# GpSimd's high and low split in two column halves, in an attention and MLP kernel

## The reference

```python
x1 = layernorm(x)                        # 16 x 512 x 128
xn = layernorm(x1) * ln_g + ln_b
q, k, v = xn @ Wq + bq, xn @ Wk + bk, xn @ Wv + bv
content = einsum("bihd,bjhd->bhij", q + u_bias, k)
pos = relative_shift(einsum("bihd,jhd->bhij", q + v_bias, pe @ Wp))
attn = softmax((content + pos) * dh ** -0.5)
head = einsum("bhij,bjhd->bihd", attn, v)
h = relu(s0 * concat([x1, -x1]) @ sign(k0)) * 2
h = relu(s1 * h @ sign(k1)) * 2
out = x + head @ Wo + bo + s2 * h @ sign(k2)
```

## Time and profile before

| what | value |
|---|---|
| time, three runs | 1454.56, 1454.69, 1456.49 us (median 1454.69) |
| the profiled execution | 1453.06 us |
| its span, first to last instruction | 1451.2 us |
| granted TensorE clock, mean | 0.998 |
| busy: PE, DVE, ACT, POOL | 1439.9, 1356.9, 1227.7, 757.3 us |
| DMA, mean over the span | 379 GB/s |

### The profile page before, as it was taken

How to read it: one execution, slowest core, us unless ns; L and a number is a source line. 1 busy time by engine, 2 the same in 40 slices (tenths; PEclk the granted TensorE clock), 3 DMA queues, 4 the chain that set the end, 5 groups by cost and what they waited for, 6 DMA issues and landing times.

```text
span 1451.2 us, 41653 instructions
## 1 busy us (share of the span) xinstructions
PE 1439.9 (99%) x16170; PEld 976.7 (67%) x16170; DVE 1356.9 (93%) x3489; ACT 1227.7 (85%) x1365; POOL 757.3 (52%) x753
## 2 busy tenths in 40 slices
PE   8999999999999999999999999999999999999999
PEld 4566666666676666666666676666766666666666
DVE  6899999999999999999999999999999999999996
ACT  5688888888888898888888888888888888888874
POOL 5565465555655566554655555466554655543410
PEclk9999999999999999999999999999999999999999
DMA  5999999999999999999999999999999999999992
GB/s 201 371 403 384 395 400 389 385 399 382 405 381 395 395 381 404 383 393 395 384 397 374 404 392 391 398 380 405 381 387 388 394 402 378 403 379 395 390 401 107
DMA packets 80867, 550.41 MB, mean 379 GB/s; under 512 B 9376, under 2 KB 10528, under 8 KB 15136
## 3 DMA queue, kind: packets, MB, share of 16 engines
q1 hardware_dynamic: 80240, 547.06, 97.2%
q10 hardware_dynamic: 432, 0.69, 0.2%
HBM read 274.57 MB, written 273.15 MB: 377 GB/s over the span
## 4 chain that ended last, share of the span: by engine, by line
PE 96%; ACT 1%; DMA 1%; DVE 1%; issue 0%; POOL 0%; SPq 0%; POOLq 0%
PE ps_pt L850 36%; PE ps_av L864 19%; PE ps_pos L826 15%; PE ps_job L753 12%; PE ps_job L717 4%; PE ps_job L707 3%; PE ps_job L732 2%; PE ps_con L838 1%; PE ps_job L728 1%; PE ps_job L740 1%; PE ps_job L723 1%; ACT pt_sb L511 1%; DMA sc_sb<-shift 1%; PE ps_job L734 0%; PE ps_job L736 0%; PE ps_pos L850 0%
## 5 line engine op out<-in xcount | busy, mean ns | idle before, releaser
L670 DVE CUSTOM_DVE_ANT_0 sc_sb<-ps_con,sc_sb 128x512 f32<-128x512 f32 x1024 | 662.2, 683 | 63.3 <-PE ps_con L838 59.6
L497 ACT COPY pos_sb<-ps_pos 128x1024 f32<-128x1024 f32 x510 | 518.4, 1016 | 179.3 <-PE ps_pos L826 172.3
L678 DVE TENSOR_SCALAR sc_sb<-sc_sb,nmax 128x512 f32<-128x512 f32 x1024 | 629.2, 646 | 0.1
L850 PE MATMUL ps_pt<-c_sb,sc_sb 128*128 128x128 f32 x4048 | 553.5, 280 | 1.9 <-ACT pt_sb L511 1.1
L511 ACT ACTIVATE pt_sb<-ps_pt 128x1024 f32<-128x1024 f32 x506 | 519.6, 1027 | 17.6 <-PE ps_pt L850 16.3
L850 PEld LDWEIGHTS ps_pt<-c_sb,sc_sb 128*128 128x128 f32 x4048 | 433.9, 141 | 126.5 <-issue 95.7
L864 PE MATMUL ps_av<-pt_sb,v_sb 128*9 128x128 f32 x8192 | 320.0, 274 | 0.1
L864 PEld LDWEIGHTS ps_av<-pt_sb,v_sb 128*9 128x9 f32 x8192 | 172.8, 90 | 184.5 <-issue 182.2
L838 PE MATMUL ps_con<-k_stack,q_stack 26*128 26x512 f32 x1024 | 265.5, 496 | 1.8 <-DVE nmax L670 1.8
L403 POOL CAST h<-act_sb 128x512 fp32r<-128x512 f32 x128 | 78.4, 612 | 357.5 <-ACT act_sb L480 355.1
L826 PE MATMUL ps_pos<-p_stack,q_stack 26*128 26x512 f32 x1024 | 259.9, 496 | 1.0 <-ACT pos_sb L497 0.7
(11 more groups left out here) (116 smaller groups left out, 1017.1 us busy)
## 6 DMA issues: line engine op xcount, KB each, us to landing
shift<-pos_sb SPq DMA_DIRECT2D x256, 1026.0 KB, 7.9
sc_sb<-shift SPq DMA_DIRECT2D x256, 1024.0 KB, 9.9
x_sb<-in_x SPq DMA_DIRECT2D x16, 256.0 KB, 9.7
out<-x_sb SPq DMA_DIRECT2D x15, 256.0 KB, 10.5
c_sb<-in_consts ACTq DMA_DIRECT2D x1, 288.0 KB, 6.9
sc_sb<-in_wp SPq DMA_DIRECT2D x1, 256.0 KB, 4.6
sc_sb<-in_stack_w ACTq DMA_DIRECT2D x1, 256.0 KB, 5.8
heads<-in_pe_t SPq DMA_DIRECT2D x1, 256.0 KB, 6.2
```

The costliest lines, as they stand in the source:

```text
L497: act.copy(to, ps_pos[:, :, :]).then_inc(s_pe, 1)
L670: dve.tensor_tensor_reduce(sc_sb[:, m % N_SC, t, :], ps_con[:, k, :], sc_sb[:, m % N_SC, t, :], -SCALE, 3.4e38, ALU.add, ALU.min, nmax[:, ...
L678: dve.tensor_scalar(sc_sb[:, m % N_SC, t, :], sc_sb[:, m % N_SC, t, :], nmax[:, m % N_SC, t:t + 1], None, ALU.subtract).then_inc(s_sub, 1)
L850: last = pe.transpose(pt_banks(k)[:, j % 2, t * P:(t + 1) * P], sc_sb[:, u % N_SC, t, j * P:(j + 1) * P], id_sb)
```

## The change

Each of the two instructions of a split is issued twice, once for columns 0 to 255 and once for 256 to 511: first both halves of the first instruction, each raising `s_pool` when done, then both halves of the second. The half of the second waits for `s_pool` to have counted the same half of the first. Only the last of the four raises `s_hl`, so consumers wait for the whole as before. The pair for `wq_hl` (L417, L418) stays whole, and nothing else is touched.

```diff
+        CUTS = (slice(0, S // 2), slice(S // 2, S))
...
-                    own(pool.tensor_tensor(dst, src, low.broadcast_to([P, S]), ALU.mult))
-                    pool.tensor_tensor(dst, src, dst.bitcast(F32), ALU.subtract).then_inc(s_hl, 1)
+                    for cut in CUTS:
+                        done[0] += 1
+                        pool.tensor_tensor(dst[:, cut], src[:, cut], low.broadcast_to([P, S // len(CUTS)]), ALU.mult) \
+                            .then_inc(s_pool, 1)
+                    for i, cut in enumerate(CUTS):
+                        pool.wait_ge(s_pool, done[0] - len(CUTS) + 1 + i)
+                        last = pool.tensor_tensor(dst[:, cut], src[:, cut], dst[:, cut].bitcast(F32), ALU.subtract)
+                    last.then_inc(s_hl, 1)
...
-                    own(pool.tensor_copy(dst[:, 0, :], src))
-                    pool.tensor_tensor(dst[:, 1, :], src, dst[:, 0, :].bitcast(F32), ALU.subtract) \
-                        .then_inc(s_hl, 1)
+                    for cut in CUTS:
+                        done[0] += 1
+                        pool.tensor_copy(dst[:, 0, cut], src[:, cut]).then_inc(s_pool, 1)
+                    for i, cut in enumerate(CUTS):
+                        pool.wait_ge(s_pool, done[0] - len(CUTS) + 1 + i)
+                        last = pool.tensor_tensor(dst[:, 1, cut], src[:, cut], dst[:, 0, cut].bitcast(F32), ALU.subtract)
+                    last.then_inc(s_hl, 1)
```

## The result

The changed kernel took 1444.45 us in the median of four executions (1442.96 to 1446.42), the kernel before 1455.49 in the same session (1454.56 to 1456.49). The ratio is 0.9924 with a 95% interval of 0.9912 to 0.9936, so 11.0 us less. The forecast was a gain of 4.4 us, 1450.3, with a range down to 1446.5. The profiled execution of the changed kernel took 1446.42 us against 1453.06: 6.6 us less. The profiled execution of before lay 2.4 us under its session's median, that of the changed kernel 2.0 over its own.

The account below looks back on a forecast made before the run. PE was taken as the bound, held up by DVE subtractions waiting for POOL. The terms -5.4 + 1.4 - 0.4 = -4.4 us gave 1448.7 from the profiled 1453.06, or 1450.3 on the median's scale; range 1446.5 to 1457.

Parts of the forecast that it names:

- What bounds it, and the link to DVE: PE, 99% busy, is the bound; POOL is off the path but delays DVE's L678, and so PE's content matmuls.
- The handover between two halves: A waiting L678 on DVE gets in between two back-to-back POOL halves, ending 0.28 us behind the first.
- rival (b): No handover between halves of one tensor, so L678 waits for both: about 1473 us; chance 0.16 including dear halves.
- The three places, 5.4 us: Content matmuls waiting for a bank behind delayed L678s: pieces of 0.26, 0.13 and 0.04 us; all gone, gaining 5.4 us.
- The 0.26 and 0.13 places: Two content matmul waits, 13 pieces each, worth 3.4 and 1.6 us in all; both expected to vanish.
- The cost of a half, +0.37 a split: Halves of 0.42 (cast), 0.64 (multiply) and 0.75 us (subtraction) on POOL make a split 0.37 us longer.
- The give-back of 1.4 us: Near 701 us, where the second L678 meets no next split, DVE and a content matmul slip 0.10 us, 14 times.
- The start, 0.4 us: From 46 to 52 us PE waits for the reduction; shorter L678 waits there were to gain 0.4 us.
- Rival (c): At the start the clock is kept up instead of falling to 1.2 GHz: 2.4 us more gain, 1448 us; chance 0.06.
- The signs named: Halves of 0.75, 0.42, 0.64 us; POOL near 860; longest L678 near 1.0, more over 0.5, sum little changed; chain pieces gone.
- the new piece near 701: A new 0.1 us wait of the content matmul in the chain, where DVE's reduction comes 0.10 us later.
- Cover for POOL's results, 1.9 us: The last L0 split of a batch ends 1.9 us before its matmuls, so a delay of some 0.6 us stays hidden.

Follow-up runs that it names:

- the narrow subtraction: Kernel before, instructions whole, but from batch 2 on the second instruction of a split subtracts only 8 of 512 columns: 1447.55 us, ratio 0.9944.
- quarters: The change with both instructions of a split in four pieces of 128 columns instead of two halves: 1463.1 us, ratio 1.0064 to the kernel before.
- the assumed sizes: The change plus one-column writes, two before the subtraction's first half and one between its halves, meant to reach the forecast's lengths: 1447.12 us, ratio 0.9940.
- thirds: The change with the `wq_hl` pair also in halves and the subtraction in pieces of 176, 168 and 168 columns: 1444.61 us, ratio 0.9927.
- the writes behind the wait: Kernel before, instructions whole, with two one-column writes after the wait for the first instruction and before the second: 1463.84 us, ratio 1.0060.
- `wq_hl` too: The change with the pair that makes `wq_hl` near 44 us in halves as well: 1443.83 us, ratio 0.9920 to the kernel before.
- the writes ahead of the wait: Kernel before, instructions whole, with two one-column writes before the second instruction's wait for the first: 1455.0 us, ratio 0.9998.

## Why the prediction was right in sign and wrong in size

The forecast was 6.6 us short of the measured 11.0. By the terms of its sum, 1.4 are a give-back that did not come, 0.9 are places that it did not count, and the largest part, some 4, is the start with its clock.

- **What bounds it, and the link to DVE.** Right: POOL off the path, the gain through L678's waits and the content matmul. The subtraction in halves alone, and the narrow subtraction, give the same 6.1 to 6.4 us in the steady part.
- **The handover between two halves.** Right, and so rival (b) was wrong: 441 of the 447 L690 that waited end some 0.28 us behind the half or other instruction that they met. It is not assured, as the five that waited for a second piece and the 5.5 us in quarters show, and the forecast had no term for that. That L678 "always" ends so was too strong for the kernel before too: of 280 that waited, 32 began inside a row normalisation (L288) and ended 0.14 us ahead of its end (the one at 80.24 us took 0.64). The Trainium skill (SBUF — State Buffer, section Who interferes with whom) has the lock held for the full instruction; the halves agree, and show that it is mostly per instruction, not per run of instructions; the L690 of 5.5 us is the exception.
- **The three places, 5.4 us.** The 0.26 and 0.13 places went as worked out. What failed is the count of places. The forecast took the third to be 8 pieces of 0.04; half steps 2 and 14 together lost 1.1 to 1.2 us. I had read the chain for pieces, and an excess of 0.05 us in a half step, spread over 14 batches, is hard to see in it; comparing each half step's duration with that of its like shows it at once. The term is some 6.3 instead of 5.4.
- **The cost of a half, +0.37 a split.** Wrong: +0.15. The step that failed is "POOL instructions have a fixed part; the nearest row for it is the 128x4 one". By the two sizes (0.40 and 0.61 us for 256 and 512 columns of the cast, 0.735 and 1.28 of the subtraction) the recorded fixed part is 0.19, and 0.045 of that lies beside the instruction before. From the 102 cycles of the Trainium skill (GPSIMD Engine Reference, section 7, Performance pitfalls for Q7 kernels), stated for a read command and not for an added instruction, I had an estimate of 0.09 for the longer split; the trace has 0.15, nearer to that than to my 0.37.
- **The give-back of 1.4 us.** Wrong, and the term with the most wrong in it. "The second instruction begins 0.15 later" measured 0.01 to 0.02 (663.96 less 663.25 is 0.71, before 0.69: a cast of 0.61 and the wait of 0.08). And the start of the first instruction was held fixed while splits that follow each other push each other: at the earlier trace rows the split starts 0.47 later and the L690 there meet other pieces. With about half of the assumed sizes put back, 3.2 us are given back, but at half steps 20 and 25, so the step named the wrong place also apart from its sizes. With the full sizes it was not measured.
- **The start, 0.4 us.** Wrong by most of what is missing. Rival (c) was this mechanism, priced at 2.4 us more, with a chance of 0.06. Its evidence stood in the profile: 6.8 us at 1.2 GHz after PE stood idle, behind waits of the very kind that the change shortens. The step that failed is to take the stretch at 1.2 GHz as nearly fixed, and as the same in all executions of a kernel. The medians contain the difference: 6.3 to 6.4 us of steady part leave 4.3 to 4.6 of the 10.7 to 11.0, and with batch 0 whole the gain is 6.7. Of what is left some 2.5 us are the clock, by the estimate from the mean clocks; the rest, with about 0.5 of earlier start in the one profile, is within the scatter of the start and stays open.
- **The signs named.** The halves' durations, POOL's busy time (by accident) and the vanished pieces came as said, the new piece near 701 did not. All L690 together take 644 us, before 662 ("little changed": too cautious), and 445 take over 0.52 us, before 306. The longest is still 1.50 instead of near 1.0: it is one at 45.2 us, behind the `wq_hl` subtraction that stayed whole, which I had forgotten.
- **Cover for POOL's results, 1.9 us.** Right for halves, and quarters show that it is one of the next limits.

## What to carry to other kernels

Where two engines exclude each other for a whole instruction, look at the one with slack and cut its instructions so that the busy one gets in between, but only as far as the slack engine's own deadline allows, and with an eye on long rows of small pieces, behind which the busy engine can wait for the whole row (5.5 us in quarters). Cut the one that is met where the bound engine has no margin, and don't let the cut delay an instruction that stays whole: here 0.06 us of delay cost 7.6 us in the steady part, where the change brings 6.3. For a forecast, compare like steps of the loop over the trace for small repeated excesses, let successive work push what follows it, and give a clock that falls after idle time at the start a term with its own chance.

## What the runs showed that was not expected

- The stretch at 1.2 GHz near 50 us came in three lengths in these profiles, by their clock records: 6.83, 3.41 and 0 us. 6.83: before, the first profile of the change, batch 0 whole, the narrow subtraction, thirds, the writes behind the wait. 3.41: halves of the subtraction alone, halves in batch 0 only, the assumed sizes, `wq_hl` too, the writes ahead of the wait. 0: the change again, halves of the first instruction alone, quarters (whose fall came at 89.2 us, for 3.41). What decides between them within one kernel stays open.
- A tie of 0.03 us between DVE and POOL went to either side, and cost PE 0.55 us when POOL got in.
- A subtraction of DVE waited 5.5 us behind a row of quarters on POOL, passing none of the ends between them.
- A POOL instruction starts 0.045 us before the recorded end of the last when it waits for nothing; a write of one column takes 0.09 to 0.10 us, a subtraction of 8 columns 0.21.
